# Attention and quantised feed-forward block: one global slot schedule, batch 0 started before the other batches are normalised, row maxima half a batch ahead

## What is computed

```python
xn = _layernorm(x)                      # (x - mean) / sqrt(var + 1e-5), per row
Q, K, V = xn @ W_q.T, xn @ W_k.T, xn @ W_v.T
Qr, Kr = rope(Q), rope(K)               # rotary embedding, pairs of dimensions
scores = einsum('bhqd,bhkd->bhqk', Qr, Kr) / 4, causal mask
attn = (softmax(scores) @ V) @ W_o.T
xq = fake_quant_fp8(xn)                 # ONE scale from max|xn| over all 8 batches
wq = fake_quant_fp8(weight)
out = x + attn + (xq @ wq.T + bias)
```

## Time and profile before

| | us |
|---|---|
| median of 3 runs | 468.52 (466.98 to 469.78) |
| the profiled execution | 468.62 |
| its span, first to last instruction | 466.9 |
| PE busy | 405.5 (87%) |
| DVE busy | 350.1 (75%) |
| ACT busy | 277.3 (59%) |
| POOL busy | 274.4 (59%) |
| mean granted TensorE clock | 0.938 |

### The profile page before, as it was taken

One profiled execution on the slowest core, in us unless ns is written; L12 is line 12 of the kernel. 1 busy time (PEld: TensorE's weight loads), 2 busy tenths in 40 slices (PEclk: granted clock), 3 DMA queues, 4 the chain that ended last, 5 costly groups with the idle time before them and its releaser, 6 DMA issues.

```text
span 466.9 us, 9145 instructions
## 1 busy us (share of the span) xinstructions
PE 405.5 (87%) x2819; PEld 222.8 (48%) x2819; DVE 350.1 (75%) x1340; ACT 277.3 (59%) x500; POOL 274.4 (59%) x278
## 2 busy tenths in 40 slices
PE   1790676999889999999999999999999999998975
PEld 1440521364345556654565556555655545643443
DVE  3779899969769977997799778977897878842041
ACT  2742932147765677567666765677567656675850
POOL 2304376636746984698459844985498337226552
PEclk9996555599999999999999999999999999999999
DMA  7826747300483238422851375037504760020021
GB/s 234 257 87 197 159 136 193 81 5 18 143 214 84 69 101 204 131 69 78 216 144 46 93 213 152 32 110 206 158 18 124 194 170 2 4 93 3 1 91 46
DMA packets 37617, 53.43 MB, mean 114 GB/s; under 512 B 5152, under 2 KB 31136, under 8 KB 37536
## 3 DMA queue, kind: packets, MB, share of 16 engines
q1 hardware_dynamic: 37568, 52.84, 40.6%
HBM read 35.78 MB, written 17.04 MB: 113 GB/s over the span
## 4 chain that ended last, share of the span: by engine, by line
PE 44%; POOL 22%; ACT 11%; issue 10%; DVE 8%; DMA 3%; POOLq 1%; SPq 1%; ACTq 0%; DVEq 0%
PE st_ps L842 10%; PE o_ps L922 9%; PE s_ps L860 7%; ACT prob L722 6%; PE m_ps L894 5%; PE m_ps L869 4%; POOL prob L427 4%; POOL rot L259 4%; PE m_ps L798 4%; POOL rot L253 3%; DVE scratch L587 3%; POOL xq L457 3%; POOL parts L263 3%; POOL rot L252 2%; POOL qv L453 2%
## 5 line engine op out<-in xcount | busy, mean ns | idle before, releaser
L587 DVE CUSTOM_DVE_ANT_0 scratch<-s_ps,causal 128x512 bf16<-128x512 f32 (+3 forms) x512 | 220.9, 485 | 55.0 <-PE s_ps L860 52.9
L722 ACT ACTIVATE prob<-st_ps 128x512 f32<-128x512 f32 x320 | 174.8, 600 | 97.9 <-PE st_ps L842 97.4
L427 POOL TENSOR_SCALAR_AFFINE_SELECT prob<-prob 128x512 f32<-128x512 f32 (+1 forms) x160 | 86.4, 544 | 130.9 <-ACT prob L722 129.4
L860 PE MATMUL s_ps<-k_st,q_st 96*128 96x512 bf16 (+3 forms) x512 | 130.8, 320 | 7.0 <-DVE rowmax L587 3.2
L842 PE MATMUL st_ps<-q_st,k_st 98*128 98x128 bf16 (+3 forms) x512 | 121.9, 303 | 4.2 <-ACT prob L722 2.8
L922 PE MATMUL o_ps<-prob,v_sb 128*17 128x512 f32 (+3 forms) x1024 | 87.4, 437 | 10.0 <-ACT heads L737 5.1
L842 PEld LDWEIGHTS st_ps<-q_st,k_st 98*128 98x128 bf16 x512 | 42.0, 97 | 76.3 <-ACT prob L722 42.3
L860 PEld LDWEIGHTS s_ps<-k_st,q_st 96*128 96x128 bf16 x512 | 48.9, 99 | 43.7 <-DVE rowmax L587 20.6
L922 PEld LDWEIGHTS o_ps<-prob,v_sb 128*17 128x17 f32 x1024 | 20.5, 96 | 48.3 <-issue 36.0
L587 DVE DVE_READ_ACCUMULATOR2_ANT rowmax<- 128x1 f32 x512 | 41.7, 81 | 0.1
L894 PE MATMUL m_ps<-wo_sb,attnT 128*128 128x256 f32 x128 | 33.2, 381 | 1.8 <-DVE x_res L610 1.4
(11 more groups left out here) (99 smaller groups left out, 502.6 us busy)
## 6 DMA issues: line engine op xcount, KB each, us to landing
qk_parts<-parts SPq DMA_DIRECT2D x16, 768.0 KB, 3.7
q_st<-qk_parts SPq DMA_DIRECT2D x32, 192.0 KB, 3.3
k_st<-qk_parts SPq DMA_DIRECT2D x32, 192.0 KB, 3.7
q_st<-x_dram SPq DMA_DIRECT2D x8, 512.0 KB, 5.5
q_st<-qk_parts SPq DMA_DIRECT2D x32, 128.0 KB, 3.4
k_st<-qk_parts SPq DMA_DIRECT2D x32, 128.0 KB, 3.7
x_res<-x_dram SPq DMA_DIRECT2D x8, 512.0 KB, 3.5
out_dram<-x_res SPq DMA_DIRECT2D x8, 512.0 KB, 4.8
```

Source lines behind the costliest of these rows:

```text
L427: eng.affine_select(out=ap, in_=ap, compare_op=ALU.is_ge, fill=0.0, base=0, pattern=pat, channel_multiplier=-1).then_inc(masked, 1)
L587: eng.tensor_tensor_reduce(scratch[:, at, col:col + w], s_ps[at][:, col:col + w], causal[:, T - w:T], 1.0, NEG, ALU.add, ALU.max, rowmax[: ...
L722: eng.activation(prob[u][:, half * T:(half + 1) * T], st_ps[ST_BANK[2 * s + half]][:, :], ACT.Exp, scale=SCALE).then_inc(exp_done, 1)
L860: mm = eng.matmul(bank[:, col:col + (qb + 1) * P], q_st[0:ROWS, 1 - par, h, qb * P:(qb + 1) * P], k_st[0:ROWS, 1 - par, h, 0:(qb + 1) * P] ...
```

## The change

The iterations are gone. There is one loop over slots from -10 to 175; a table says at which offset from 20n an item of batch n stands. With `LEAD = 10` the maxima of batch n are computed in slots 20n-10 to 20n+9. The prologue holds batch 0 and the normalisation of batch 1; the others are normalised at `LATE_NORM`. The fp8 scale is known at slot 18, so the quantisation of xn starts with batch 0 at slot 23. For batches 4 to 7 the sums come from ACT (`accum_out`) in place of DVE's `bn_stats`. x is loaded into `xnT` itself and normalised in place, in memory of its own.

```diff
-MISC = [(0, "mt", 1), (0, "v", 0), (1, "qk", 0), (2, "qk", 1), (3, "v", 1), (4, "qk", 2), (5, "o", 0),
+LEAD = 10
+OFFSETS = {("v", 0): 0, ("mt", 1): 1, ("v", 1): 2, ("o", 0): 23, ("o", 1): 24, ("o", 2): 25, ("mt", 2): 6, ("o", 3): 26,
...
+           ("at", 3): 31, ("fin", 2): 32, ("qk", 1): -28, ("qk", 2): -26, ("fin", 3): 34, ("qk", 3): -24, ("mt", 0): -4}
+SPREAD = [(17, "spread", 0, 0), (18, "spread", 0, 1)]
+LATE_NORM = {2: -8, 3: -6, 4: -4, 5: -1, 6: 5, 7: 9}
+ACT_NORM = 4
...
+            def read_stack(n, w, i):
+                eng.wait_ge(parts_out[w], 16 * (n + 1))
+                if n >= 2:
+                    eng.wait_ge(st_full, HALVES * (n - 2) + HALVES // 2 * (i + 1))
...
-                eng.dma_start(shift_dram[half_].rearrange("t a n -> a t n"), shift[:, :, :])\
-                   .then_inc(shift_out[half_], 16)
-                eng.wait_ge(shift_out[half_], 16 * (n + 1))
...
+            def shift_rows(n, g):
+                c = NG * n + g
+                eng.wait_ge(shift_done, c + 1)
+                for t in range(SHIFT):
+                    eng.dma_start(q_st[ROWS + t:ROWS + t + 1, n % 2, g * HG:(g + 1) * HG, :],
+                                  shift[:, t, :]).then_inc(shift_in[c % 2], 16)
...
+            def store(n):
...
+                    for qb in range(NQ):
+                        eng.wait_ge(fin_done, 4 * n + qb + 1)
+                        eng.dma_start(to[:, qb, :], x_res[:, qb, :]).then_inc(y_out, 16)
...
+            for slot in range(FIRST_SLOT, END_SLOT):
+                for off, g in ((-3, 0), (2, 1), (7, 2), (12, 3)):
+                    n = batch_at(slot, off)
+                    if n is not None:
+                        shift_rows(n, g)
...
+                if slot in range(1, 2 * NB, 2):
+                    largest(slot // 2)
+                weight_step(slot)
...
+            def add_up(n):
+                p = n % 2
+                eng.wait_ge(x_in[n], 16)
+                wait_past(eng, ln_square, NQ * (n - ACT_NORM))
+                for t in range(NQ):
+                    eng.activation(unread[:, t, :], x_of(n)[:, t, :], ACT.Identity, accum_out=sums[:, p, t:t + 1])\
+                       .then_inc(ln_sum, 1)
+
+            def add_squares(n):
+                p = n % 2
+                eng.wait_ge(ln_mean, n - ACT_NORM + 1)
+                for t in range(NQ):
+                    eng.activation(unread[:, t, :], x_of(n)[:, t, :], ACT.Square, bias=nmean[:, p, t:t + 1],
+                                   accum_out=squares[:, p, t:t + 1]).then_inc(ln_square, 1)
...
+            for slot in range(FIRST_SLOT, END_SLOT):
+                at = exponent_slot(slot)
+                if at is not None:
+                    exp(*at)
+                for n, at_slot in LATE_NORM.items():
+                    if n >= ACT_NORM and slot == at_slot - 5:
+                        add_up(n)
+                    if n >= ACT_NORM and slot == at_slot - 3:
+                        add_squares(n)
+                    if slot == at_slot - 1:
+                        normalise(n)
```

More of the change, by code:

```diff
@@ L61, in wait_past @@
         eng.wait_ge(sem, count)
-def each_batch(eng, step, between):
-    for n in range(NB):
-        step(n, n % 2)
-        between(n)
 def unit_parts(u, half):
@@ new lines, in _ @@
+            eng.dma_start(bias_sb[:, :], bias.partition_broadcast(P)).then_inc(w_in, 16)
+            for w in range(2):
+                write_parts(0, w)
+            for i in range(2):
+                for w in range(2):
+                    read_stack(0, w, i)
+            for slot in range(FIRST_SLOT, END_SLOT):
[3 more added lines that the diff above has]
+                        shift_rows(n, g)
+                n = batch_at(slot, 35)
+                if n is not None and n < NB - 1:
+                    store(n)
+                n = batch_at(slot, -22, 1)
+                if n is not None:
+                    write_parts(n, 0)
+                n = batch_at(slot, 19)
+                if n is not None:
+                    load_residual(n)
+                n = batch_at(slot, -20, 1)
+                if n is not None:
+                    read_stack(n, 0, 0)
+                n = batch_at(slot, -17, 1)
+                if n is not None:
+                    write_parts(n, 1)
+                    read_stack(n, 0, 1)
+                n = batch_at(slot, -15, 1)
+                if n is not None:
+                    read_stack(n, 1, 0)
+                n = batch_at(slot, -12, 1)
+                if n is not None:
+                    read_stack(n, 1, 1)
@@ L974, in _, with scores @@
-            run(iteration)
+            def scores(n, s, between):
+                g, u = divmod(s, 5)
+                if u == 0:
+                    c = NG * n + g
+                    eng.wait_ge(shift_in[c % 2], 32 * (c // 2 + 1))
+                for half in range(2):
+                    i = 2 * s + half
+                    wait_past(eng, exp_done, HALVES * n + ST_BEFORE[i] + 1)
+                    for j, kb, col in unit_parts(u, half):
+                        h = g * HG + j
+                        mm = eng.matmul(st_ps[ST_BANK[i]][:, col:col + T - kb * P],
+                                        k_st[0:ROWS + SHIFT, n % 2, h, kb * P:(kb + 1) * P],
+                                        q_st[0:ROWS + SHIFT, n % 2, h, kb * P:T], start=True, stop=True)
+                    mm.then_inc(st_full, 1)
+                    if half == 0:
+                        between()
```

1042 lines of the change are left out of this document (499 added, 543 removed).

## The result

The changed kernel takes 531.37 us (median of 4 runs, 530.18 to 536.42); the kernel before, on the same chip, 468.04 us. The ratio is 1.137, with a 95% interval of 1.129 to 1.145. I had forecast 455.5 us in a range of 444 to 465 and 88% for faster, so the prediction was wrong in sign, by 76 us. The profiled execution took 530.18 us with a span of 528.5.

What follows compares the result with a forecast made beforehand. PE was taken to bound the main part; chains, DVE and low clock the start and tail. 66 + 54 + 48 + 4 x 47.2 + 42.3 + 39.7 + 15 = 453.8 us, plus 1.7: 455.5, range 444 to 465.

Steps and rivals of the forecast that it cites:

- Part 1: Start of the kernel: with only batch 0's chain ahead, first maxima start at 39.5 us in place of 58.10.
- the landing, 3.7 + 1 us: Start: a 192 KB key read lands after 3.7 us, plus 1 us for half stacks of twice that size.
- Part 2: Ten slots of maxima alone before batch 0: they take 26.5 us, first exponential at 66 in place of 90.45.
- the rival of the slow clock: Start and batch 0: PE stays at the low clock, ten slots take 32 us, total 463; chance 17%.
- 5 us after the start: Ten slots before batch 0: ACT's list begins 5 us in, after DVE's maxima and statistics and POOL's inverse root.
- Part 3: Slots 0 to 19, batch 0: 40.7 + 7.8 ACT + 4 DVE + 1.9 PE transposes, so 54 us, from 47 to 60.
- Seven bursts: 14.8 - 7 = 7.8: Batch 0: ACT's normalisation of batches 6 and 7 adds 14.8 us, each 2 us burst hiding about 1 us.
- Part 4: Slots 20 to 159: batch 1 takes 48 us, four batches 47.2, then 42.3 and 39.7; moved projections cost nothing.
- Part 5: Shift rows, slot 1 to slot 5: direct transfers are hidden in 9.4 us of room and change nothing of the sum.
- the rival on the other side: Shift rows become the wait: 1 us for each of 28 groups, total 483; chance 9%.
- Part 6: Tail: 15 us in place of 17.9, about 1.5 from earlier quantisation and bias, last store taken at 1.4.
- The balance rival: Bursts hide in batch 0 and even projections close two PE gaps in five batches: total 444; chance 17%.

Runs made afterwards that it cites:

- run 4: Changed kernel with second-half stack reads moved behind the fourth shift, quantisation one slot earlier, and statistics of batches 4 to 7 back on DVE: 505.25 us, 1.077 of before.
- run 13: The seventh run's kernel with batches 6 and 7 normalised in batch 1 and two of the eight largest-magnitude reductions left out: 483.64 us, 1.032 of before.
- the seventh run: The sixth run's kernel with ACT's multiplication one slot earlier and three long POOL operations each in its own slot: 482.36 us, 1.027 of before.
- runs 10 and 11: The seventh run's kernel with eight DVE reductions reading 8 elements per row, 479.89 us; or with four of them, in full, moved ahead of batch 0, 485.39 us.
- Runs 5, 6 and 7: On run 4's kernel, cumulatively: quantisation spread over more slots, 494.82 us; first output transposes in slot 7, 485.65 us; long POOL operations apart, 482.36 us.
- run 1: Changed kernel with the reads of the second half stacks moved to slot 12, behind the fourth shift of the batch before: 510.60 us, 1.088 of before.
- run 8: Kernel before, with only its shift rows sent straight SBUF to SBUF in two small transfers per half batch: 468.67 us, 1.000 of before.
- run 2: Changed kernel with the quantisation of xn one slot earlier, away from POOL's last subtraction: 528.43 us, 1.126 of before.
- the sixth run: Run 4's kernel with quantisation spread over more slots, plus the first attention-output transposes moved from slot 6 to 7: 485.65 us, 1.035 of before.
- runs 2 to 4: Changed kernel with quantisation one slot earlier, 528.43 us; with moved stack reads too, 511.46 us; with statistics of batches 4 to 7 also on DVE, 505.25 us.

## Why the prediction was wrong

- **Part 1, the first maxima** (39.5, measured 42.6). The issue of the key reads was forecast from 33.4 to 34.7 and stood from 34.23 to 35.46. The term that failed is the landing, 3.7 + 1 us; the keys were there 7.1 us after, with one set of half stacks ahead of them on the queue and two behind. Within the range of 37 to 44.
- **Part 2, the first exponential** (66, measured 72.9; 30.3 us against 26.5 for the ten slots). At the upper edge of its range of 60 to 73. The term that failed is where ACT's list begins: "5 us after the start" was 9.8, behind DVE's statistics and POOL's inverse root. The list itself took 72.9 - 52.4 = 20.5 us, where I had 21.5. With the accumulator read a sum took 0.41 us from start to start, less than the 0.52 I had taken, so counting it at nothing was right. PE's clock had a mean of 0.78 here, so the rival of the slow clock had a share in this; what that cost in this stage no run separates.
- **Part 3, batch 0** (54, measured 66.8; 62.5 from slot 1 to 21). The mis-sized term is that of ACT's bursts, "Seven bursts: 14.8 - 7 = 7.8", half of them hidden. The part of it that run 4 took back, the sums and squares, gave 8.0 us alone, and what is left of it, the normalisations with their transposes and two reductions, took 10.5 in run 13. Taken together, an estimate across two kernels, that is 18.5 where 7.8 + 1.9 = 9.7 stood. In the changed kernel PE waited 3.1 and 4.1 us in this stretch for ACT's normalise and its copies, at a mean clock of 0.86. The reductions were within 4 us, measured 2.2. Missing were the scale chain's waits on PE, 1.8 and 1.1 us in the seventh run, with work at a clock of 0.73 behind them. The rival that it is DVE which holds this batch fell in runs 10 and 11.
- **Part 4, the steady batches** (47.2, measured 54.5 to 58.9; with batches 1 and 6 this is 52.7 of the 74.7 us by which the span was off). This is the step that failed most: "The price of the projections moved from slots 1 to 6 to slots 10 to 16 is nothing, as PE stays the bound". I priced items, and not what stood beside them in a slot. The other engines' totals per batch hardly changed (DVE 39.48 and 41.88, ACT 31.18 and 31.35). What changed is which operations share a slot of 2.4 us, with two banks each for scores and for the shared work: both quantisation steps with a row of splits and maxima, the transposes with the maxima's split. Runs 5, 6 and 7 moved only such places and gave 23 us. No run put the projections back into slots 1 to 6, so what that move costs by itself is not shown.
- **Part 5, the shift rows** (hidden, with four slots of room). They became a wait, and the rival on the other side had its place right ("behind 768 KB of stacks on one queue"). Its price was 1 us for each of 28 groups; it was up to 3.2 for one group, the third, in each of five batches. What failed is "four slots, 4 x 2.36 = 9.4 us" against a landing of at most 6.0: that group had 6.5 us and a landing of up to 8.4. Moving the reads gave 20.8 us (run 1), and the same part in the kernel before costs nothing (run 8). So the transfers are not at fault, but the order of the reads ahead of them.
- **Part 6, the tail** (15, measured 16.6). From the end of the last exponential the kernel before took 18.6 (448.3 to 466.9), so 2.0 us came of the 1.5 + 1.4 that were forecast.

In the rivals, one sum doesn't close: two gaps in five batches are 7.5 us, and 5.5 was taken off. The balance rival would be 442. It changes nothing here, where the time lies far on the other side.

The ledger by medians: 531.4 us; the queue 20.8, the slot of run 2 on top of it -0.9, the statistics 6.2, and the three slots 10.4 + 9.2 + 3.3. That is 49 of the 76 us by which I was off, and leaves 482.4. (By the ratios, times 469, the terms are 22.9, -1.8, 7.0, 9.5, 10.3 and 3.8.) Why that version is not at 455.5 is known by stage and only in part by cause. Its first exponential comes at 74.9 (forecast 66), batch 0 and batch 1 take 60.6 and 52.2 (54 and 48), and each of four later batches 1.7 more than 47.20. Of the 1.7 the four small transposes of maxima, in place of two, are 2 x 0.27 = 0.5; the rest I can't name.

The mechanism that I had left out altogether is what a wait does afterwards. In the trace of before a fall to half clock stood only at the start, and I priced it only there. In the changed kernel it follows each wait of 2.0 to 3.2 us: 12.4 us of waiting removed gave 20.8 us of time, a factor of 1.7. It does not follow a single wait of 1.14 us, and there the factor is small: in the sixth run 8.0 gave 9.2. The line between them is not sharp. In runs 2 to 4 the clock fell after some of the 1.64 us waits and not after others, and in run 2 it stayed at 1.00 behind one of 2.93.

The Trainium skill (SBUF — State Buffer, SBUF: two separate sides) has one port pair that GpSimd shares with those DVE instructions that run in a two-port mode or read two inputs from SBUF: whichever starts first holds it for the whole instruction, and the other is fully blocked. The second wait agrees: 2.57 us beside POOL's subtraction and 0.67 away from it. By the rule alone, undoing the overlap gives back 1.9 us in each of five batches, some 9.5 us by my estimate; run 2 gave 2.9 in all, not clear of noise, so the duration followed the rule and the time did not.

## What to carry to other kernels

Before moving work between slots of a schedule that runs at its bound, list for each slot what every engine and every queue has in it, and compare the longest engine of the slot with the slot's length; equal totals per batch did not show the 11 us here. Price a wait of an engine that bounds the kernel above its own length where the trace shows the clock fall after it, here at 1.7 times for waits of 2 to 3 us, and near its own length where the clock stays whole, as after 1.15 us here. For a small transfer with a deadline, read what is issued on its queue in the microseconds ahead of it, and not only its room in slots.
